# Last norm run one row tile behind its gate, with early table loads, a halved last store and a Newton inverse root in the first norm

## The reference

```python
h = x @ W; al, ar = h @ a_l, h @ a_r                     # attention layer
e = exp(-leaky_relu(al[src] + ar[dst], 0.1))
h_prime = segment_sum(e * h[dst], src) / (segment_sum(e, src) + 1e-5)
x = layernorm(x + elu(h_prime))                          # "the first norm"
u = x @ root + bias + sum_r mean_r(x[src]) @ weight[r]   # 8 relations
z = concat([u, x]) @ w_gate + b_gate
h = tanh(u) * z + x * (1 - z)
out = layernorm(x + h)                                   # "the last norm"
```

## Time and profile before

| what | us |
|---|---|
| median of 3 runs | 1059.75 |
| the profiled execution, its own time | 1058.46 |
| span in its profile | 1056.7 |
| PE busy | 1019.6 (96%) |
| DVE busy | 329.4 (31%) |
| ACT busy | 279.8 (26%) |
| POOL busy | 253.8 (24%) |

### The profile page before, as it was taken

One profiled execution on the slowest core, in us unless ns is written; L12 is line 12 of the kernel. 1 busy time (PEld: TensorE's weight loads), 2 busy tenths in 40 slices (PEclk: granted clock), 3 DMA queues, 4 the chain that ended last, 5 costly groups with the idle time before them and its releaser, 6 DMA issues.

```text
span 1056.7 us, 14898 instructions
## 1 busy us (share of the span) xinstructions
PE 1019.6 (96%) x5414; PEld 857.9 (81%) x5414; DVE 329.4 (31%) x707; ACT 279.8 (26%) x478; POOL 253.8 (24%) x196
## 2 busy tenths in 40 slices
PE   7899889999999999999999999999999999999995
PEld 5677667878898897898888888888889889888874
DVE  6866874531120220220220211202202202112285
ACT  4322443761212221221211122112212212222422
POOL 0000001036413113122222132131231221326720
PEclk9999999999999999999999999999999999999998
DMA  6223435156311411321321221230041041212302
GB/s 239 70 84 103 141 115 183 55 192 168 101 41 41 133 50 40 123 61 40 111 71 40 102 81 41 74 108 26 16 162 39 21 160 33 70 49 70 121 1 97
DMA packets 63622, 91.81 MB, mean 87 GB/s; under 512 B 4116, under 2 KB 30179, under 8 KB 63429
## 3 DMA queue, kind: packets, MB, share of 16 engines
q1 hardware_dynamic: 63556, 90.86, 27.1%
HBM read 75.17 MB, written 15.67 MB: 86 GB/s over the span
## 4 chain that ended last, share of the span: by engine, by line
PE 89%; DVE 5%; ACT 3%; issue 1%; DMA 1%; SPq 0%; DVEq 0%; POOL 0%; ACTq 0%
PE ps L1082 20%; PE ps L1084 19%; PE ps L1083 19%; PE ps L1287 9%; PE ps L1288 9%; PE ps L1156 5%; PE ps L1276 2%; PE ps L1123 2%; DVE ps L1024 1%; DMA xT_raw<-xT 1%; DVE ps L1023 1%; DVE oh_s L757 1%; PE ps L1131 1%; PE ps L1133 0%; PE ps L1132 0%
## 5 line engine op out<-in xcount | busy, mean ns | idle before, releaser
L422 POOL TENSOR_TENSOR w_lo<-w_raw,w_hi 128x512 fp32r<-128x512 f32 x168 | 216.9, 1296 | 754.8 <-ACT w_hi L497 581.7
L497 ACT CAST w_hi<-w_raw 128x512 fp32r<-128x512 f32 x184 | 114.3, 621 | 471.5 <-PE ps L1084 398.8
L1082 PE MATMUL ps<-w_hi,M_hi 128*128 128x512 f32 (+1 forms) x560 | 221.7, 396 | 13.2 <-DVE w_lo L751 7.5
L1084 PE MATMUL ps<-w_lo,M_hi 128*128 128x512 f32 (+1 forms) x560 | 218.7, 391 | 0.0
L1083 PE MATMUL ps<-w_hi,M_lo 128*128 128x512 f32 (+1 forms) x560 | 218.6, 390 | 0.0
L974 DVE SCALAR_TENSOR_TENSOR u<-ps,scale,u 128x512 f32<-128x512 f32 (+1 forms) x90 | 66.4, 744 | 427.6 <-PE ps L1084 427.6
L1287 PE MATMUL ps<-C_hi,x_hi 128*128 128x320 f32 (+3 forms) x640 | 189.2, 313 | 0.0
L1288 PE MATMUL ps<-C_hi,x_lo 128*128 128x320 f32 (+3 forms) x640 | 187.9, 311 | 0.0
L1083 PE MATMUL ps<-w_hi,M 128*128 128x512 f32 (+1 forms) x360 | 142.4, 396 | 0.0
L1084 PE MATMUL ps<-w_lo,M 128*128 128x512 f32 (+1 forms) x360 | 142.3, 395 | 0.0
L1082 PE MATMUL ps<-w_hi,M 128*128 128x512 f32 (+1 forms) x360 | 142.1, 395 | 0.0
(11 more groups left out here) (152 smaller groups left out, 754.6 us busy)
## 6 DMA issues: line engine op xcount, KB each, us to landing
w_raw<-weights SPq DMA_DIRECT2D x184, 256.0 KB, 2.9
C_dram<-Cst SPq DMA_DIRECT2D x25, 512.0 KB, 6.3
C_hi<-C_dram SPq DMA_DIRECT2D x8, 1600.0 KB, 7.2
z<-b_gate SPq DMA_DIRECT2D x5, 512.0 KB, 9.8
u<-bias SPq DMA_DIRECT2D x5, 512.0 KB, 7.3
xT_raw<-xT SPq DMA_DIRECT2D x8, 312.5 KB, 8.1
u<-x SPq DMA_DIRECT2D x4, 512.0 KB, 5.1
last_raw<-weights SPq DMA_DIRECT2D x8, 256.0 KB, 6.2
```

Source lines behind the costliest of these rows:

```text
L422: pool.tensor_tensor(w_lo[k % RING][:, :], w_raw[k % RING][:, :], w_hi[k % RING][:, :].bitcast(f32), ALU.subtract).then_inc(w_lo_done, 1)
L497: nc.scalar.copy(w_hi[k % RING][:, :], w_raw[k % RING][:, :]).then_inc(w_hi_done, 1)
L1082: mm(o, lhs_hi[:, k, c], w_hi[k % RING][:, :], start=opens, stop=False)
L1084: last = mm(o, lhs_hi[:, k, c], w_lo[k % RING][:, :], start=False, stop=closes_)
```

## The change

Four parts. (1) In the last norm DVE normalizes tile 0 after the gate of tile 1, tiles 1 and 2 after the gate of tile 2, and tile 3 between the two last quarters of tile 4. (2) ACT runs a Sqrt on a spare column after the last Exp of the first norm and after the last Tanh, so that Sqrt's table is loaded there. (3) The last tile is normalized and stored in two halves of 512 columns. (4) In the first norm the inverse root of tiles 2 and 3 is made on DVE, by a first guess from the bits and three Newton steps, instead of by ACT's Sqrt; with it the order of PE's items and the banks of three transposes change.

```diff
         def x1T_pair(t):
-            return (1, 0, 3, 1, 3)[t]
+            return (1, 0, 1, 3, 2)[t]
@@ sync
-            sp.wait_ge(y2_done, NT)
             even = rows(NT - 1) // 16 * 16
-            for r0, r1 in ((0, even), (even, rows(NT - 1))):
-                sp.dma_start(out[P * (NT - 1) + r0:P * (NT - 1) + r1, :], u[r0:r1, NT - 1, :]).then_inc(out_done, 16)
-            sp.wait_ge(out_done, 16 * (NT + 1))
+            for half in range(2):
+                c = slice(half * H2, (half + 1) * H2)
+                sp.wait_ge(y2_done, NT + half)
+                for r0, r1 in ((0, even), (even, rows(NT - 1))):
+                    sp.dma_start(out[P * (NT - 1) + r0:P * (NT - 1) + r1, c], u[r0:r1, NT - 1, c]).then_inc(out_done, 16)
+            sp.wait_ge(out_done, 16 * (NT + 3))
@@ scalar
+            act.wait_ge(eps_set, 1)
...
             square(3)
-            std(2, 4)
             exp_relu(4)
+            nc.scalar.activation(spare_col[:, 0:1], eps_col[:, :], ACT.Sqrt)
             x1T_high(2)
             x1T_high(3)
             square(4)
...
             for t in range(2, NT):
                 tanh(t)
+            nc.scalar.activation(spare_col[:, 1:2], eps_col[:, :], ACT.Sqrt)
@@ vector
-            v.memset(eps_col[:, :], EPS)
+            v.memset(eps_col[:, :], EPS).then_inc(eps_set, 1)
...
+            def inverse_std(t0, t1):
+                guess = rstd[:, t0:t1]
+                dve.wait_ge(y_sq_done, t1)
+                step(v.tensor_scalar(root_of[:, :], y_sq[:, t0:t1], 1.0 / D, EPS, ALU.mult, ALU.add))
+                step(v.tensor_scalar(root_bits[:, :], root_of[:, :].bitcast(i32), 1, None, ALU.arith_shift_right))
+                step(v.tensor_scalar(guess.bitcast(i32), root_bits[:, :], -1.0, 1597463007.0, ALU.mult, ALU.add))
+                for _ in range(3):
+                    step(v.tensor_tensor(root_part[:, :], root_of[:, :], guess, ALU.mult))
+                    step(v.scalar_tensor_tensor(root_part[:, :], root_part[:, :], -0.5, guess, ALU.mult, ALU.mult))
+                    step(v.scalar_tensor_tensor(guess, root_part[:, :], 1.5, guess, ALU.add, ALU.mult))
...
+            def inverted_std(t0, t1, batch):
+                dve.wait_ge(std_done, batch)
+                step(v.reciprocal(rstd[:, t0:t1], rstd[:, t0:t1]))
...
-            normalize(0, 2, 1)
+            inverted_std(0, 2, 1)
+            normalize(0, 2)
             add_elu(3)
             x1T_low(0)
             x1T_low(1)
-            normalize(2, 4, 2)
+            inverse_std(2, 4)
+            normalize(2, 4)
             add_elu(4)
             x1T_low(2)
             x1T_low(3)
-            normalize(4, NT, 3)
+            inverted_std(4, NT, 2)
+            normalize(4, NT)
@@ vector, last norm
-                normalized(t, h_neg_mean[r, t:t + 1], ALU.add)
+                if t in (1, 2):
+                    normalized(t - 1, h_neg_mean[0:rows(t - 1), t - 1:t], ALU.add)
+                if t == 2:
+                    normalized(t, h_neg_mean[r, t:t + 1], ALU.add)
             r = slice(0, rows(NT - 1))
-            for q in range(2, 4):
-                gate_quarter(q, last_bank(NT - 1) + q - 2, 0)
+            gate_quarter(2, last_bank(NT - 1), 0)
+            normalized(NT - 2, h_neg_mean[:, NT - 2:NT - 1], ALU.add)
+            gate_quarter(3, last_bank(NT - 1) + 1, 0)
             v.bn_aggr(mv[r, NT - 1, :], quarters[r, :, :]).then_inc(var_done, 1)
-            normalized(NT - 1, mv[r, NT - 1, 0:1], ALU.subtract)
+            dve.wait_ge(std2_done, NT)
+            step(v.reciprocal(rstd[r, NT - 1:NT], rstd[r, NT - 1:NT]))
+            for half in range(2):
+                c = slice(half * H2, (half + 1) * H2)
+                v.tensor_scalar(u[r, NT - 1, c], u[r, NT - 1, c], mv[r, NT - 1, 0:1], rstd[r, NT - 1:NT], ALU.subtract, ALU.mult)\
+                 .then_inc(y2_done, 1)
@@ tensor
             for k in range(RING):
                 z_items(k, (0, 1))
                 if k == 1:
+                    turn_x1(2)
+                if k == 2:
                     pe.wait_ge(hp_read, 4)
-                    turn_x1(2)
                     turn_x1(3)
+            pe.wait_ge(x1T_lo_done, 3)
+            for k in range(RING):
+                z_items(k, (2,))
+            pe.wait_ge(hp_read, NT)
+            turn_x1(4)
             pe.wait_ge(x1T_lo_done, 4)
             for k in range(RING):
-                z_items(k, (2, 3))
-                if k == 1:
-                    turn_x1(4)
+                z_items(k, (3,))
             pe.wait_ge(x1T_lo_done, NT)
-            pe.wait_ge(hp_read, NT)
             for k in range(RING):
                 z_items(k, (4,))
```

More of the change, by code:

```diff
@@ L85, in gat_rgcn_kernel @@
         dots = sb("dots", [P, 4 * NT], f32)
+        root_of = sb("root_of", [P, 2], f32)
+        root_bits = sb("root_bits", [P, 2], i32)
+        root_part = sb("root_part", [P, 2], f32)
+        spare_col = sb("spare_col", [P, 2], f32)
         key = sb("key", [P, ALL_TILES], f32)
@@ L177, in x1T_pair @@
         def x1T_pair(t):
-            return (1, 0, 3, 1, 3)[t]
+            return (1, 0, 1, 3, 2)[t]
+        eps_set = sem("eps_set")
         edges_here = sem("edges_here")
@@ L931, in add_elu, with normalize @@
                 v.tensor_scalar(neg_mean[r, t:t + 1], y_sum[r, t:t + 1], -1.0 / D, None, ALU.mult).then_inc(y_done, 1)
-            def normalize(t0, t1, batch):
+            def inverse_std(t0, t1):
[9 more added lines that the diff above has]
+            def inverted_std(t0, t1, batch):
                 dve.wait_ge(std_done, batch)
                 step(v.reciprocal(rstd[:, t0:t1], rstd[:, t0:t1]))
+            def normalize(t0, t1):
                 for t in range(t0, t1):
```

## The result

Over 20 runs each, the changed kernel has a median of 1056.55 us (1049.38 to 1058.89), the kernel before 1061.99 (1055.8 to 1065.26); the ratio is 0.9933, with a 95% interval of 0.9915 to 0.9950. So it is faster by 0.5 to 0.85%, against 0.62% forecast. The two medians themselves differ by 5.44 us, or 0.51%, near the lower end of that interval. The absolute 1053.1 was 3.45 us too low, mainly because it stood on a median of three runs, which were among the lower ones: the median of 20 is 2.24 us above it.

What follows compares the result with a forecast made beforehand. PE bounds the kernel (89% of the span), so time comes only from its waits or what follows its last matmul. Last norm 4.8 + halved store 0.3 + first norm 1.5 = 6.6 us; 1059.75 - 6.6 = 1053.1, range 1050.5 to 1056.0.

Steps and rivals of the forecast that it cites:

- the signs that it listed: Last norm: last scaling 2.8 us after PE's last matmul ends, end of span 6.9 us after it, in place of 12.
- Last norm, 4.8: Last norm: normalizing one tile behind starts the last scaling at 1047.52 in place of 1052.33, 4.8 us.
- Early table: Last norm: spare Sqrt after last Tanh takes the 1.28 load off tile 0's root, within the 4.8.
- PE's end is the floor: Last norm: DVE is free when the last quarter comes; slip of scaling 3 or its root costs 0.1 to 0.5 us.
- Halved store, 0.3: End of last norm: storing the last tile in halves ends at 1051.6 against 1051.9 whole, 0.3 us; bounds +0.7 and -0.4.
- First norm, 1.5: First norm: PE's next round after the first starts at 218.8 in place of 220.31, 1.5 us; bounds 0.9 to 1.6.
- The rival in which the Newton chain eats all of it: First norm gives nothing if Newton steps take over 0.31 us; 5.1 us left, 1054.7; chance 10%.
- The level: Whole kernel: absolute median of 1053.1 us, from 1059.75 less 6.6; range 1050.5 to 1056.0.

## Why the prediction was right, and where not

The sum was 4.8 + 0.3 + 1.5 = 6.6 us; the stretches gained 6.34, the runs 0.67% (0.50 to 0.85), and their medians 5.44 us. Of the signs that it listed, the last scaling starts 2.72 us after PE's last matmul ends (2.8 was put) and the span ends 6.97 us after it (6.9).

- **Last norm, 4.8.** The places came as laid out: waits for PE at tiles 2 and 3 and at the third quarter (the first of its half), one hidden wait for ACT at tile 2. The last quarter was put at 30.80 us after the first gate and came at 30.98, since PE was slower. The last matmul ends 30.94 us after the first gate in the changed kernel, and 30.94 or 30.95 in all twelve later traces, where the trace of the kernel before has 1044.74 - 1014.04 = 30.70. Why PE was slower there stays open. "PE's end is the floor" held: the quarter starts 0.04 us after it, and DVE was free at 1049.29, so the two arrive together, as the text had it. The term measured 35.61 - 30.98 = 4.63.
- **Early table.** "Part of the 4.8, since DVE then waits for PE anyway" is shown by the run without it: its last stretch is as long as in the changed kernel, to 0.04 us.
- **Halved store, 0.3.** Over-sized: 0.11. The half scaling at 0.54 us was right (0.55). The step that failed is the transfer, of which 0.7 us was said to be saved: from the issue of SP's second pair at 1053.27 to the end at 1056.23 it took 2.96, where 3.54 - 0.7 = 2.84 was put, and the whole store took 1056.66 - 1053.16 = 3.50 before; so 0.54 was saved. The reading behind the 0.7 was off too. It let 0.46 MB move at the first half microsecond's 311 GB/s, in 1.4 us, with 1.1 after the last byte. The packets of that store run from 1054.00 to 1055.92, 1.92 us, and 0.74 is left behind them. The 2.0 us and 436 GB/s that the prediction quotes from the Trainium skill (DMA: Bandwidth & Descriptors, "Anatomy of one DMA") are a fit for DMAs issued on the gpsimd path, and the stores here are SP's.
- **First norm, 1.5.** 1.64. The chain took 2.36 us where 2.3 was put, PE waited 0.21 where 0.1 was put, and still it is more: PE's four gaps of the stretch (transposes and waits with the step into the next item) shrank from 5.27 us to 3.74, 1.53, and the 56 plain steps from one matmul to the next gave the other 0.11, 0.234 us each in place of 0.236. The rival in which the Newton chain eats all of it needed 0.31 us a step; the run with six steps, the same 1.8 us longer in all, shows that its mechanism was right and only its condition wasn't met.
- **What the text got wrong in its weighing.** It told the first norm as ACT's detour taken off the chain. The runs with one of the two show that PE's order, which lets tile 2 go ahead of tile 3, is worth 1.16 together with the early table of tile 4's root, and the Newton root 0.50.
- **The level.** The measured 1056.55 lies above the stated 1050.5 to 1056.0; the measured ratio on the prediction's own base gives 1059.75 x 0.9933 = 1052.6, inside it. The step that failed here is the base: the median of three runs was 2.24 us low, and the other 1.2 us are the 6.6 less the 5.44 of the medians. The text took the scatter of the median for about 1.5 us; the scatter is made of clock falls of about 1.5 or 3 us each, one to seven of them in the traces, and three runs don't average them. That 0.67% came so close to the 0.62% forecast is partly luck, as the interval of the ratio alone is 3.7 us wide; the 6.34 us of the stretches bear the sum out.

## What to carry to other kernels

Where the whole time scatters by more than an edit is worth, compare stretches between fixed places of the program in single traces: here they repeat to about 0.1 us while the runs spread over 10. Before making a chain of steps faster, look at the order in which its results are used: letting one tile through early, with an early table load for the last tile, won twice as much as taking a root and two table loads off ACT. And price an early table load by the wait that would follow it: it was worth 1.27 us in one order and nothing in another.

## What the runs showed of the hardware

TensorE's granted clock fell from 2.4 to 1.2 GHz for 3.4 or 6.8 us at a time. In the relation steps PE had been busy without a gap for the 10 us before each fall. In the changed kernel's trace a fall began inside the 40 transposes near 178 us, before which PE had waited 0.81 us, and at the two-column rows of five of the eight relation steps; in the kernel before at three of eight, and not near 178. Over the 20 runs of the changed kernel the whole execution follows it: the span was 1047.6 us at a mean clock of 0.994 and 1057.0 at 0.984. The chance of a fall is not explained by any run here. Breaking the row of small matmuls up did not stop the falls. The small DVE instructions of 128 x 2, each awaited, came 0.197 us apart, `scalar_tensor_tensor` as fast as `tensor_tensor`. Behind an ACT_TABLE_LOAD the next function started 1.29 to 1.30 us after the load's start (217.12 to 218.42) in every case but the load at the very start of the kernel, where it waits for its data. ACT's instruction before that load ended at 217.10, so the further drain that the Trainium skill has for it (ScalarE: Activation LUTs, "What ACT_TABLE_LOAD costs") does not show here, on either side of the load.
